# An attention and mixture kernel: at the turn from gather to scatter, VectorE takes one of two evictions of four units, and a wait of ScalarE is taken out

## The reference

```python
grouped = x.reshape(b, s // g, g, d)                        # groups of g = 32 tokens
logits = jnp.einsum('bntd,des->bntes', grouped, Wc) + bc    # plus a small tie breaker
perm = (logits == jnp.max(logits, axis=-3, keepdims=True))  # each expert picks one token of a group
permuted = jnp.einsum('bntd,bntes->bnesd', grouped, perm)                           # gather
inner = jax.nn.relu(jnp.einsum('bnesd,esdf->bnesf', permuted, W1) + b1)             # 32 inner values
result_permuted = jnp.einsum('bnesf,esdf->bnesd', inner, W2) + b2
result = jnp.einsum('bnesd,bntes->bntd', result_permuted, perm)                     # scatter
```

## Time and profile before

| | |
|---|---|
| median of 3 runs | 2923.41 us (2923.05 to 2923.77) |
| profiled execution | 2926.86 us, span 2925.1 us |
| mean granted TensorE clock | 0.988 |
| TensorE busy | 2769.8 us (95%) |
| VectorE busy | 2053.4 us (70%) |
| ScalarE busy | 1715.0 us (59%) |
| GpSimd busy | 1463.4 us (50%) |
| moved by DMA | 316.37 MB, mean 108 GB/s |

### The profile page before, as it was taken

One profiled execution on the slowest core, in us unless ns is written; L12 is line 12 of the kernel. 1 busy time (PEld: TensorE's weight loads), 2 busy tenths in 40 slices (PEclk: granted clock), 3 DMA queues, 4 the chain that ended last, 5 costly groups with the idle time before them and its releaser, 6 DMA issues.

```text
span 2925.1 us, 135112 instructions
## 1 busy us (share of the span) xinstructions
PE 2769.8 (95%) x59836; PEld 2237.4 (76%) x59836; DVE 2053.4 (70%) x2871; ACT 1715.0 (59%) x3424; POOL 1463.4 (50%) x2319
## 2 busy tenths in 40 slices
PE   8999999999999999999999999999677787899998
PEld 7888888888888888888888888887566676455554
DVE  6777777777777777777777777777444443788998
ACT  5666566566666666656656656665333333666674
POOL 4666666666667667666666666666110000111111
PEclk9999999999999999999999999999899998899999
DMA  4222222222222222222222222222644443578776
GB/s 154 78 73 69 74 78 76 73 78 77 72 79 74 72 82 73 73 77 74 75 75 78 74 72 79 76 73 58 215 132 136 110 123 119 178 222 269 234 228 195
DMA packets 262711, 316.37 MB, mean 108 GB/s; under 512 B 28000, under 2 KB 184032, under 8 KB 260464
## 3 DMA queue, kind: packets, MB, share of 16 engines
q1 hardware_dynamic: 252176, 297.55, 33.7%
q10 hardware_dynamic: 9952, 10.17, 1.1%
HBM read 194.31 MB, written 113.31 MB: 105 GB/s over the span
## 4 chain that ended last, share of the span: by engine, by line
PE 89%; DVE 4%; issue 4%; DMA 1%; SPq 1%; POOL 1%; ACT 0%; ACTq 0%; DVEq 0%; POOLq 0%
PE a_proj L991 41%; PE a_mix L991 12%; PE s_ps L1714 6%; PE g_pick_ps L1465 6%; PE a_scan L1105 5%; PE s_ps L1735 4%; DVE g_picked L1394 3%; PE s_ps L1730 3%; PE a_scan L1082 3%; PE a_scan L1069 2%; PE g_acc_ps L1489 2%; PE a_mix L1057 2%; PE a_misc L1049 1%; PE a_misc L1123 1%; DMA part_dram<-res 1%
## 5 line engine op out<-in xcount | busy, mean ns | idle before, releaser
L991 PE MATMUL a_proj<-wdh,xTh 128*128 128x512 f32 x1024 | 421.2, 411 | 5.5 <-issue 3.7
L991 PE MATMUL a_proj<-wdh,xTl 128*128 128x512 f32 x1024 | 402.4, 393 | 0.3 <-issue 0.3
L991 PE MATMUL a_proj<-wdl,xTh 128*128 128x512 f32 x1024 | 400.0, 391 | 1.7 <-issue 1.7
L823 DVE COPY_PREDICATED scan_in<-mask,a_scan 64x512 f32<-64x512 uint32 x512 | 382.4, 747 | 16.1
L1671 ACT COPY s_stage<-s_ps 128x1024 f32<-128x1024 f32 x256 | 279.2, 1147 | 150.9 <-PE s_ps L1714 142.4
L464 POOL TENSOR_TENSOR dx<-xs,d_row 64x512 f32<-64x512 f32 x256 | 331.4, 1294 | 15.1
L472 POOL TENSOR_TENSOR yv<-yt,dx 128x512 f32<-128x512 f32 x128 | 189.0, 1476 | 293.2 <-DVE yt L863 293.2
L639 ACT ACTIVATE scan_in<-CT,hsel 64x128 f32<-64x128 f32 x1024 | 326.2, 388 | 4.8
L603 ACT ACTIVATE raw<-a_proj,rs 128x272 f32<-128x272 f32 x128 | 62.5, 488 | 427.4 <-PE a_proj L991 427.4
L1394 DVE COPY g_picked<-g_pick_ps 128x1024 f32<-128x1024 f32 x128 | 156.7, 1224 | 218.4 <-PE g_pick_ps L1465 218.4
L1691 DVE STREAM_TRANSPOSE s_turned<-s_stage 128x2048 f32<-128x2048 f32 x128 | 294.4, 2302 | 9.8 <-ACT s_stage L1671 9.8
(11 more groups left out here) (152 smaller groups left out, 7275.3 us busy)
## 6 DMA issues: line engine op xcount, KB each, us to landing
x<-in_x_dram SPq DMA_DIRECT2D x128, 256.0 KB, 2.7
xn_dram<-xn SPq DMA_DIRECT2D x128, 256.0 KB, 2.4
part_dram<-res SPq DMA_DIRECT2D x128, 256.0 KB, 2.5
g_xn<-xn_dram SPq DMA_DIRECT2D x512, 64.0 KB, 2.3
s_part<-part_dram SPq DMA_DIRECT2D x128, 256.0 KB, 4.1
out_dram<-s_out SPq DMA_DIRECT2D x128, 256.0 KB, 3.8
xr<-in_xT_dram SPq DMA_DIRECT2D x126, 256.0 KB, 2.9
s_inner<-inner_dram SPq DMA_DIRECT2D x32, 512.0 KB, 4.1
```

The lines of the kernel that those rows point to most:

```text
L823: nc.vector.copy_predicated(dst, mask[rows_, :].unsqueeze(1).unsqueeze(1).to_broadcast([CH, 4, 2, CH]), src).then_inc(mt_cp, 1)
L991: last = nc.tensor.matmul(out, lhs[a], rhs[c], start=(k == 0 and n == 0), stop=(k == nk - 1 and n == 2))
```

## The change

VectorE copies the second pair (h = 1) of units 0 to 3, in a new function `move`, and counts it with a new semaphore `w2_mv`. ScalarE copies only the first pair of these units. VectorE's moves stand in its program ahead of the two last clamps, two and two. The thresholds of TensorE's and VectorE's waits follow. ScalarE's wait for the inner stores ahead of unit 4 is taken out.

```diff
         scatter["rest_b2"](dve)
         for i in range(2):
+            for u in range(2 * i, 2 * i + 2):
+                scatter["move"](dve, u)
             clamp_acc(NGB - 1, i)
...
+    SHARED = QB
...
-        for h in range(2):
+        for h in range(1 if u < SHARED else 2):
             nc.scalar.copy(places[:, h, :, :, :], bank[:, pair(u, h), :, :]).then_inc(w2_cp, 1)
 
+    def move(dve, u):
+
+        m, i = divmod(u, QB)
+        dve.wait_ge(w2_ps, u + 1)
+        places = stage[m % 2][:, 4 * i:4 * i + 4, :, :].rearrange("p (j h) d r -> p h r j d", h=2)
+        nc.vector.tensor_copy(places[:, 1, :, :, :], bank[:, pair(u, 1), :, :]).then_inc(w2_mv, 1)
+
     def scalar_program(act):
-        for i in range(2):
-            act.wait_ge(gat["inner_out"][i], gat["inner_count"] * (NGB // 2))
         for u in range(4, UNITS):
             evict(act, u)
...
+        dve.wait_ge(w2_mv, SHARED)
         for m in range(STEPS):
-            dve.wait_ge(w2_cp, 2 * QB * (m + 1))
+            dve.wait_ge(w2_cp, 2 * QB * (m + 1) - SHARED)
...
-        wait(pe, w2_cp, 2 * u if u < 4 else 2 * u - 1)
+        if u < SHARED:
+            wait(pe, w2_cp, u)
+            wait(pe, w2_mv, u)
+        elif u == SHARED:
+            pe.wait_ge(w2_cp, u)
+        else:
+            pe.wait_ge(w2_mv, SHARED)
+            pe.wait_ge(w2_cp, 2 * u - 1 - SHARED)
```

More of the change, by code:

```diff
@@ L1561, in scatter_phase @@
     w2_cp = sem("w2_cp")
+    w2_mv = sem("w2_mv")
     turn_cp = sem("turn_cp")
@@ L1747, in scatter_phase @@
     return dict(sync=sync_program, gpsimd=gpsimd_program, scalar=scalar_program, vector=vector_program, tensor=tensor_program,
-                load_first=load_first, apply_w2=apply_w2, evict=evict, round_b2=round_b2, rest_b2=rest_b2)
+                load_first=load_first, apply_w2=apply_w2, evict=evict, move=move, round_b2=round_b2, rest_b2=rest_b2)
 def program(nc, io):
```

## The result

The changed kernel takes 2931.35 us in the median of 17 runs (2923.68 to 2943.23), the kernel before 2923.77 (2921.06 to 2930.44) beside it. The ratio is 1.0026, with a 95% interval of 1.0015 to 1.0038: slower by about 7.6 us, where 6.0 us of gain were forecast. The profiled execution took 2929.62 us.

What follows compares the result with a forecast made beforehand. TensorE, holding 89% of the chain of waits, was taken as the bound. Gains of 1.3 + 4.2 + 0.45 = 5.95, about 6.0 us, gave 2920.9 us profiled and 2917.4 us median; range 2913.2 to 2920.8 us.

Steps and rivals of the forecast that it cites:

- The bound: Whole kernel: TensorE holds 89% of the chain of waits, so its standing still or running at lower clock is what counts.
- all of that steady part shifts with W2(8), whatever its date: Steady scatter, 120 units at 3.13 us each: the whole part moves with the start of unit 8's W2 matmuls.
- Covered edits: VectorE's new wait for its own copies, changed thresholds, first-step transposes and part loads: claimed to cost nothing.
- Two engines evict units 0 to 3: Start of the turn: sharing copies removes TensorE's waits ahead of W2 in units 1 to 3; gain 1.3 us.
- The low bound: Shared evictions in units 0 to 3: gain only 0.60 us if W1's issue gaps swallow all but the first wait.
- Rival 2: Turn: instruction supply paces the first units and the clock returns late; gain 3.0 us, time 2920.4; chance 0.17 with another rival.
- The wait for the inner stores: Unit 4 of the turn: ScalarE evicts without waiting; gain 4.2 us, bounds 3.3 and 4.2, plus 0.45 for unit 5's clock.
- The clock's return: First scatter units after the turn: full clock may come back later, 2.2 us more at half clock costing 0.9 us.
- my low end: Turn: 0.6 + 3.3 = 3.9 us, less 0.9 us for the clock, leaving a gain of 3.0 us.
- the 3.0 to 6.0 that I had worked out for the turn: Turn: gain from 3.0 us, the low case, to about 6.0 us, the forecast sum.
- rival 3: Behind the turn: without unit 4's pause, TensorE's instruction queue can't catch up; stops of 2.8 to 3.7 us, 2928.5; chance 0.03.

## Why the prediction was wrong

- **The bound, and "all of that steady part shifts with W2(8), whatever its date"**: right about the unit (3.13 us in both), wrong about the part. It stopped for 13.7 us before and for 22.3 after.
- **"Covered edits ... the changed thresholds, cost nothing: the data are long there"**: this is the step that failed. The wait on VectorE's moves is met, so nothing waits for it. But in three of four units it makes one more instruction, and it pushed the late wait off the weight load. The same wait alone costs the kernel before 0.29%, and with it taken out from unit 6 on the loss is gone (0.9990). I had counted the engine's waits and not its instructions, though the diff shows the `else` branch in all 123 remaining units. The gain of the turn was 4 us, the price of this line some 8 to 11.
- **Two engines evict units 0 to 3**: VectorE's copy was 1.23 us for 1.22, covered as said. The gain was 0.6 us in the first trace of the change and none in the second (17.0 us both), for 1.3. The low bound, "0.60 if they swallow all but the first", was the right value, or still too high, and its reason, the supply of instructions, was the right one. Rival 2 held for this term.
- **The wait for the inner stores**: 6.85 us became 2.76, that is 4.1, for 4.2. W2(4) and W2(5) ran at full clock; I had counted half of the second.
- **The clock's return**: it took 1.1 us back (W2(8) to W2(10) 8.65 us, 7.54 before), near the 0.9 of my low end. From W2(0) to W2(10) the change saves 42.1 - 37.8 = 4.3 us, inside the 3.0 to 6.0 that I had worked out for the turn.
- **The rivals**: rival 3 had the sign and the symptom, stops of TensorE for issue behind the turn, with a chance of 0.03, and the wrong cause. It also had them longer and fewer: of the 11 stops one was of the 2.8 to 3.7 us that it named. The pause at unit 4 is not what keeps them away: with the pause put back the kernel is as slow, and with the pause gone and one wait it has no more stops than before. What was missing is a rival that asks what each unit's added instruction does to a queue that is short of supply, which the gaps of the earlier trace rows had shown.
- **What stays open**: in the profiled executions the change is 2.7 us behind, in the medians 7.6; traces of one execution don't resolve a difference of 0.3%. The kernel with the wait alone taken out gains 8 us in the medians, while its turn saves 3.5 and its stops don't fall. The rest isn't located; the part ahead of W2(0) varies by more than that from trace to trace. How the cost splits between the number of instructions and the late wait standing apart is not settled either, since their intervals overlap, nor why such an instruction makes a fetch start later.

## What to carry to other kernels

Ask of every wait that an edit leaves in a loop whether it is needed there each time: where a semaphore only counts up, a wait that an engine has once passed stays met for it, so it belongs at its first use alone. Where two waits must stand ahead of one instruction, see in the trace which of them becomes an instruction of its own, and let the late one ride. And where a profile shows stops called issue, the instruction supply is a resource like any other: a wait removed ahead of it gives less than its own length, and added instructions cost though nothing waits for them.

## What the runs showed of the hardware

TensorE's instructions came in blocks of 256 (16.4 KB a packet). With weight loads and small matmuls back to back, one block came in 3.4 to 3.9 us in the turn (mean of two, 14 traces). The steady scatter needs one in some 4.7 us, and there 8 to 13 of some 78 blocks were still late: their fetch had started 2.2 to 6.5 us behind the border before, instead of 1.2 to 1.5, and TensorE went on 2.2 to 2.8 us after its start. The place of these stops moved by two units when a 512 KB load did. After a stop of 2.78 us the granted clock was 0.62 over 4.4 us, and the unit lost 4.8 us in all. A semaphore instruction met long ago ended 0.97 us ahead of the weight load behind it; one that was met late ended 0.40 us ahead of it and cut the queue's lead to that.
